# Projecting the leftover channels for both row halves side by side, and splitting the second chunk in the first slot

## What is computed

```python
# L0: 32 -> 192 -> 192 -> 32 channels, w1, w2, w3 ternarized (delta = 0.7 mean|w|)
h = relu6(bn(conv1x1(x, w1)))
h = relu6(bn(conv3x3(h, w2)))          # the largest part of the work
x = x + bn(conv1x1(h, w3))             # the projection
# L1: two 3x3 convolutions, 32 -> 32, weights and activations rounded to 8 bits
out = relu(bn(conv3x3(q(x), q(w1))))
x = relu(bn(conv3x3(q(out), q(w2))) + x)
# L2, L3: relu(bn(conv3x3(x, w) + b)), a channel whose largest value is under 1e-3 is set to zero
```

## Time and profile before

| | us |
|---|---|
| median of 3 runs | 267.81 |
| range of these | 267.43 to 267.94 |
| profiled execution | 268.13 |
| its span, first to last instruction | 266.3 |
| TensorE busy | 234.2 |
| VectorE busy | 233.2 |
| ScalarE busy | 184.2 |

### The profile page before, as it was taken

One profiled execution on the slowest core, in us unless ns is written; L12 is line 12 of the kernel. 1 busy time (PEld: TensorE's weight loads), 2 busy tenths in 40 slices (PEclk: granted clock), 3 DMA queues, 4 the chain that ended last, 5 costly groups with the idle time before them and its releaser, 6 DMA issues.

```text
span 266.3 us, 5565 instructions
## 1 busy us (share of the span) xinstructions
PE 234.2 (88%) x2151; PEld 133.3 (50%) x2151; DVE 233.2 (88%) x466; ACT 184.2 (69%) x274; POOL 8.7 (3%) x26
## 2 busy tenths in 40 slices
PE   0659999099999989999998999999997999789982
PEld 0315555056555445655454555555643555446651
DVE  3799989927999899999989999889878948999994
ACT  5799896348666467866458757969342747997962
POOL 4400000000000000000000000000000000000003
PEclk9999999859999999999999999999999999999997
DMA  7327100200002100001200000000000000254306
GB/s 238 99 62 241 40 1 15 75 2 0 2 0 70 25 0 2 1 2 32 60 2 0 4 0 0 2 2 1 0 2 1 2 0 0 55 118 103 88 19 241
DMA packets 7098, 10.72 MB, mean 40 GB/s; under 512 B 2176, under 2 KB 5216, under 8 KB 7072
## 3 DMA queue, kind: packets, MB, share of 16 engines
q1 hardware_dynamic: 6880, 10.33, 14.1%
q10 hardware_dynamic: 192, 0.04, 0.1%
HBM read 4.04 MB, written 1.61 MB: 21 GB/s over the span
## 4 chain that ended last, share of the span: by engine, by line
DVE 37%; PE 34%; issue 11%; ACT 8%; DMA 5%; SPq 3%; DVEq 0%; ACTq 0%
PE ps L533 10%; PE ps L522 5%; PE ps L708 4%; PE ps L544 4%; DVE hs L1251 3%; DVE h2a L1299 3%; PE ps L555 3%; DVE ps L1278 3%; DVE hs L1243 2%; DMA big<-w2b_in 2%; PE ps L643 2%; DVE h2a L1294 2%; DVE big L1587 1%; DVE cmx L1632 1%; DMA xk<-xpart 1%
## 5 line engine op out<-in xcount | busy, mean ns | idle before, releaser
L533 PE MATMUL ps<-vv,w2at 128*128 128x378 f16 (+1 forms) x192 | 38.2, 336 | 0.6 <-DVE ps L1278 0.6
L828 ACT ACTIVATE ra<-ps,bn 128x392 f32<-128x392 f32 x32 | 21.4, 675 | 19.9 <-PE ps L479 19.2
L522 PE MATMUL ps<-vv,wu 128*128 128x392 f16 x180 | 34.8, 329 | 0.0
L746 PE MATMUL ps<-big,wst 128*32 128x378 f16 (+10 forms) x576 | 24.5, 326 | 3.6 <-DVE big L1587 2.2
L533 PEld LDWEIGHTS ps<-vv,w2at 128*128 128x128 f16 x192 | 17.9, 99 | 15.8 <-issue 5.1
L708 PE MATMUL ps<-qi,wqi 128*128 128x378 bf16 (+7 forms) x144 | 23.9, 325 | 0.6 <-ACT qi L1027 0.6
L522 PEld LDWEIGHTS ps<-vv,wu 128*128 128x128 f16 x180 | 17.4, 98 | 12.1 <-DVE vv L1261 0.2
L860 ACT ACTIVATE hs<-ug,magic 128x784 f16<-128x784 f16 x16 | 15.2, 948 | 11.1 <-DVE ug L1232 11.1
L874 ACT ACTIVATE r2a<-ps,bn 128x784 f32<-128x784 f32 x15 | 15.1, 1003 | 10.7 <-DVE h2a L1299 10.7
L746 PEld LDWEIGHTS ps<-big,wst 128*32 128x32 f16 x576 | 15.2, 96 | 13.0 <-issue 2.2
L533 PE MATMUL ps<-vv,w2bt 128*128 128x378 f16 (+1 forms) x96 | 21.2, 330 | 0.0
(11 more groups left out here) (218 smaller groups left out, 443.6 us busy)
## 6 DMA issues: line engine op xcount, KB each, us to landing
xk<-xpart SPq DMA_DIRECT2D x45, 49.0 KB, 1.9
xin<-x_in SPq DMA_DIRECT2D x4, 392.0 KB, 3.8
big<-part SPq DMA_DIRECT2D x25, 49.0 KB, 2.0
big<-big SPq DMA_DIRECT2D x3, 392.0 KB, 3.6
y_out<-xin SPq DMA_DIRECT2D x3, 392.0 KB, 2.4
big<-w2a_in SPq DMA_DIRECT2D x3, 288.0 KB, 4.3
big<-w2b_in SPq DMA_DIRECT2D x6, 144.0 KB, 4.0
y_out<-xin SPq DMA_DIRECT2D x2, 196.0 KB, 2.4
```

The costliest lines, as they stand in the source:

```text
L522: i = nc.tensor.matmul(landing(slice(0, P), PBANK[k], dx), weights(raw, mid, k, dx, False), moving(s, k, dx, b), start=(n == 0 and dx == D ...
L533: i = nc.tensor.matmul(landing(slice(0, P), PBANK[k], dx), weights(raw, mid, k, dx, False), moving(s, k, dx, b), start=False, stop=(n == 2 ...
L746: i = nc.tensor.matmul(img(ps[C * g:C * g + C, bank + h, :W * n], n)[:, to[0], to[1]], wst[:, layer, C * t:C * t + C], kst[:, KBUF[layer][ ...
L828: nc.scalar.activation(ra[:, 0, HALF * h:HALF * h + HALF], ps[:, bank, :HALF], ACT.Relu, bias=bn[:, BSH, BN1A:BN1A + 1], scale=bn[:, BSC, ...
```

## The change

Four things are different.

1. Chunk 1 is split in slot 0: `x_high(1, 0)` behind the relu_main halves of image 2, `x_high(1, 1)` behind `relu_a(0)`, `split_second(1)` behind `split_first(1)`. Before, they stood between slots 0 and 1 and in slot 1.
2. A third group of semaphores, `s_second`, counts the transfers of a chunk's second image; `s_xk` counts the last two images. `expand_rest` of the first pair waits for the first two images alone, that of the second pair for the last two; the waits of `expand_main` on transfers go, but for image 2.
3. On ScalarE, `relu_main(j+2, 0)` of slots with g = 1 comes behind `relu_b(j-1)` and `copy_y(j)`, and `add_shift(c)` behind `relu_rest(j+3, 0)`.
4. `project(c, banks)` does both halves: all `h2a` steps of h = 0, those of h = 1, and then the `h2b` steps with the halves in turn, h = 1 two images on, so that neighbouring matmuls use different halves of the array's rows and different columns. It signals `proj_done` once, and both residuals wait for it.

```diff
-XK = [16 * 3 * (G - 2)] + [16 * 3 * (G - 1)] * (NCH - 1)
+XK = 16 * 3 * (G - 2)
...
                 for g in range(0 if c else 1, G):
+                    landed = s_first[c] if g == 0 else s_second[c] if g == 1 else s_xk[c]
                     for k in range(3):
                         sp.dma_start(xk[C * k:C * k + C, G * c + g, :],
-                                     xpart[C * g:C * g + C, c % 2, k, :]).then_inc(s_first[c] if g == (0 if c else 1) else s_xk[c], 16)
+                                     xpart[C * g:C * g + C, c % 2, k, :]).then_inc(landed, 16)
...
             def expand_main(j, h):
 
                 if h == 0:
-                    if j >= G and j % G == 0:
-                        pe.wait_ge(s_first[j // G], 48)
-                    if j == 2 or j >= G and j % G == 1:
-                        pe.wait_ge(s_xk[j // G], XK[j // G])
                     if j == 2:
+                        pe.wait_ge(s_xk[0], XK)
                         pe.wait_ge(rb_ready, 4)
...
             def expand_rest(j, h):
 
                 if h == 0:
-                    if j >= G and j % G == 0:
+                    if j % G == 0:
                         pe.wait_ge(s_first[j // G], 48)
-                        pe.wait_ge(s_xk[j // G], XK[j // G])
+                        pe.wait_ge(s_second[j // G], 48)
+                    else:
+                        pe.wait_ge(s_xk[j // G], XK)
                     pe.wait_ge(ra_ready, 2 * j if j > 2 else 6)
...
-            def project(c, h, steps=(0, 1, 2, 3), bank=7, end=False):
-
-                if bank == 6 and not end:
+            def project(c, banks, end=False):
+
+                if not end:
                     pe.wait_ge(ra_ready, 2 * (G * (c + 1) + 2) + 2)
-                wait(pe, y0_ready, (2 * c + h if end else 2 * c) if bank == 7 else 0)
-                lower = slice(HB * h, HB * h + HB)
-                for s in steps:
-                    if s == 0:
-                        pe.wait_ge(h2a_ready, (c + 1) * G + (h if end else 0))
-                    if s == (2 if end else 1):
-                        pe.wait_ge(h2_ready, (c + 1) * G)
-                    for g in range(G):
-                        w, rhs = ((w3t[:, 0, :], h2a[:, g, s, HALF * h:HALF * h + HALF]) if s < 2 else
-                                  (w3t[lower, 1, :], h2b[lower, g, s - 2, :]))
-                        i = nc.tensor.matmul(ps[C * g:C * g + C, bank, :HALF], w, rhs, start=(s == steps[0]),
-                                             stop=(s == steps[-1]))
+                wait(pe, y0_ready, 2 * c)
+                for h in range(2):
+                    pe.wait_ge(h2a_ready, (c + 1) * G + (h if end else 0))
+                    for s in range(2):
+                        for g in range(G):
+                            nc.tensor.matmul(ps[C * g:C * g + C, banks[h], :HALF], w3t[:, 0, :],
+                                             h2a[:, g, s, HALF * h:HALF * h + HALF], start=(s == 0), stop=False)
+                pe.wait_ge(h2_ready, (c + 1) * G)
+                for s in range(2):
+                    for k in range(G):
+                        for h in range(2):
+                            g = (k + 2 * h) % G
+                            lower = slice(HB * h, HB * h + HB)
+                            i = nc.tensor.matmul(ps[C * g:C * g + C, banks[h], :HALF], w3t[lower, 1, :],
+                                                 h2b[lower, g, s, :], start=False, stop=(s == 1))
                 i.then_inc(proj_done, 1)
...
-                    project(c - 1, 0, bank=6)
-                    project(c - 1, 1)
+                    project(c - 1, (6, 7))
...
-            project(NCH - 1, 0, end=True)
-            project(NCH - 1, 1, (2, 3, 0, 1), bank=6, end=True)
+            project(NCH - 1, (7, 6), end=True)
...
-                    if ahead and not even:
+                    if ahead and g == G - 1:
                         relu_main(j + 2, 0)
                     relu_b(j - 1)
                     copy_y(j)
-                    if ahead and even:
+                    if ahead and g < G - 1:
                         relu_main(j + 2, 0)
...
-                dve.wait_ge(proj_done, 2 * c + h + 1)
+                dve.wait_ge(proj_done, c + 1)
```

More of the change, by code:

```diff
@@ L209, in conv_seq @@
         s_first = [sem(f"s_first{c}") for c in range(NCH)]
+        s_second = [sem(f"s_second{c}") for c in range(NCH)]
         s_xk = [sem(f"s_xk{c}") for c in range(NCH)]
@@ L258, in wait, with spread_landed @@
                 eng.wait_ge(s, n)
+        def spread_landed(eng, c):
+            if c:
+                eng.wait_ge(s_first[c], 48)
+            eng.wait_ge(s_second[c], 48)
+            eng.wait_ge(s_xk[c], XK)
         def stack_free(eng, layer, c):
@@ L456, in expand_one @@
                 if n == 0:
-                    pe.wait_ge(s_first[0], 48)
+                    pe.wait_ge(s_second[0], 48)
                 nc.tensor.matmul(ps[:, bank, :HALF], (w1t[:, 0:P], w1t[:, P:P + 2 * HB])[two],
@@ L786, in x_high @@
                 if c >= 2:
-                    act.wait_ge(s_first[c - 2], 48)
-                    act.wait_ge(s_xk[c - 2], XK[c - 2])
+                    spread_landed(act, c - 2)
                 act.wait_ge(*((s_x[c], 16) if k == 0 else (xr_ready, c + 1)))
@@ L921, in slot @@
                 if begin:
+                    x_high(1, 0)
                     relu_rest(j + 2, 0)
@@ L937, in slot @@
                 relu_a(j)
-                if not begin:
+                if begin:
+                    x_high(1, 1)
+                else:
                     copy_m1(j + 1)
@@ L944, in slot @@
                     integer_block(after, 3)
+                if not even and j + 3 < B:
+                    relu_rest(j + 3, 0)
                 if g == 1:
                     add_shift(c)
-                if not even and j + 3 < B:
-                    relu_rest(j + 3, 0)
             act.wait_ge(bn1_ready, 1)
@@ L996, in _ @@
             slot(0, 0, first=True)
-            x_high(1, 0)
-            slot(0, 1, first=True, split=(1, 1))
+            slot(0, 1, first=True)
             slot(0, 2, first=True, split=(2, 0))
@@ L1159, in split_second @@
                 if c >= 2:
-                    dve.wait_ge(s_first[c - 2], 48)
-                    dve.wait_ge(s_xk[c - 2], XK[c - 2])
+                    spread_landed(dve, c - 2)
                 tt(xpart[:, c % 2, 2, :], xrest[:], high(xrest[:]), ALU.subtract).then_inc(x_split, 1)
@@ L1343, in slot @@
                     if g == 1:
-                        wait(dve, proj_done, 2 * c)
+                        wait(dve, proj_done, c)
                     upper_a(j - 1, (g - 1) % G)
@@ L1351, in slot @@
                     split_first(1)
+                    split_second(1)
                 if ahead and not even:
@@ L1434, in _ @@
             slot(0, 0, first=True)
-            split_second(1)
             slot(0, 1, first=True)
```

## The result

The changed kernel takes **258.92 us** (median of 4 runs, 258.72 to 259.40); the kernel before, timed beside it, 267.88 us (4 runs, 267.43 to 268.01). The ratio is 0.9671, with a 95% interval of 0.9653 to 0.9689. The forecast was 258.8, with a range of 257.0 to 261.8. The profiled execution took 259.40 us, with a span of 257.6, against 268.13 before. Two executions of the experiments fell in a slower state, 278.95 us of the variant with less VectorE work and 265.62 us of the one with the groups alone; the ratios leave such executions out.

The account below looks back on a forecast made before the run. It took TensorE and VectorE, both 88% busy, as nearly full, with VectorE setting the time up to the last slots and TensorE at the end. -7.67 - 2.58 + 0.39 + 0.88 = -8.98 us gave 258.8 us, range 257.0 to 261.8.

Parts of the forecast that it names:

- grid_main of image 4, VectorE: Slot 2: VectorE gets there 7.67 us earlier, 6.95 of waits, 0.63 from slot 1, 0.1 of rounding.
- VectorE's waits in g = 1: Slots (1,1), (2,1), (3,1): waits of 0.78, 0.78 and 1.02 us go with ScalarE's new order, 2.58 us off.
- add_shift: ScalarE, relu_rest ahead of it: TensorE's 0.93 us waits count nothing, as VectorE sets the time; bounds 0 and 1.9.
- projection inside: Three projections in the loop, each 0.54 us shorter, all eaten by TensorE's wait for the residual: 0, bounds 0 and 1.6.
- TensorE behind at the end: Last slots: TensorE's matmuls set the time; VectorE is 10.25 us early, TensorE only 9.86, so 0.39 back.
- signal at the end: Last projection: residual(3,0) waits for one signal behind everything, 0.88 us back; bounds 0.8 and 1.0.
- The hole: TensorE idle 6.42 us before chunk 1's first use, then some 2.9 us lost by the low clock; both would go.
- The wait in slot 1: TensorE's second expand_main waits about 0.55 us, as relu_main(3,0) ends at 42.45 behind relu_b and copy_y.
- Rival 1: Only the hole is repaid; the 0.78 and 1.02 us waits return as waits for relu_main: 261.0 us, chance 0.20.
- rival 3: Projection: row halves drain at each alternation, 1.65 us per projection: 263.2 us, chance 0.05.
- Rival 4: Slower than before: the clock falls behind four TensorE waits of 0.55 to 1.1 us: 270.4 us, chance 0.02.
- rival 2: Chunk 1's first use: TensorE's idle time shrinks but the clock still falls, costing 2.9 us: 261.7 us, chance 0.08.

Follow-up runs that it names:

- variant with less VectorE work: Changed kernel with the last projection as before, and without VectorE's second subtraction for chunks 2 and 3: 256.50 us, ratio 0.9561.
- groups alone: Kernel before with only the third group of semaphores, so expand_rest of image 4 waits for six transfers instead of twelve: 263.86 us, ratio 0.9864.
- two orders: Changed kernel's sixteen h2b matmuls with halves in turn, against a run with all h = 0, then all h = 1: 258.80 us in a single run.
- early split alone: Kernel before with only the split of chunk 1 moved into slot 0; TensorE still waits for all twelve transfers: 260.11 us, ratio 0.9724.
- filled hole: Kernel before with 34 matmuls of zeros into an unused bank ahead of TensorE's wait for chunk 1's transfers: 266.98 us, ratio 0.9960.
- late split: Changed kernel with chunk 1 split where it was before, behind slot 0 and in slot 1: 259.99 us, ratio 0.9731.
- GpSimd variant: Changed kernel with the last projection as before, and VectorE's four subtractions for chunks 2 and 3 on GpSimd: 259.86 us, ratio 0.9702.

## Why the prediction was right, point by point

The forecast was 258.8 and the result 258.92. The steps were right in kind, but that they agree to 0.1 us is luck in part. The medians give a gain of 8.96 us for 8.98 forecast, with some 0.5 us either way by the interval. The traces give 9.36 us up to the first residual of the end, 0.4 more than forecast, and the start-up that ran 0.66 us later hid it in the profiled execution. Shifts below are between the two traces, with the 0.66 us added.

| step | forecast | measured |
|---|---|---|
| grid_main of image 4, VectorE | -7.67 | 61.99 to 54.87: -7.78 |
| VectorE's waits in g = 1 | -2.58 | all three gone; undone, 2.1 us |
| L1297 of slot (3,1), both together | -10.25 | 178.60 to 168.61: -10.65 |
| add_shift | 0 | 0 (258.87 without it) |
| projection inside | 0 | about -0.25, at the third |
| TensorE behind at the end | +0.39 | -10.65 to -10.27 at the last `h2a`: +0.38 |
| signal at the end | +0.88 | +0.91 |
| first residual of the end | -8.98 | 200.43 to 191.73: -9.36 |

- **The hole.** The spread starts at 38.79 - 0.66 = 38.13, where 38.2 was forecast, TensorE waits for no transfer, and the clock does not fall behind it. The low clock's price in it was 2.72 us, forecast 2.9. The wait in slot 1 is 0.27 us instead of 0.55, and nothing hangs on it.
- **relu_b and copy_y first.** Rival 1 fell, since no wait for `ra` takes the place of the old ones. The one wait of VectorE for `ra` in the loop, 0.33 us at 158.47, is not new: the kernel before has the same 0.33 us at 167.37. Of the 1.02 us in slot (3,1), which the prediction put on this order whole, 0.24 belong to the projection, as the run with the relus in their old order shows.

- **add_shift.** The value, nothing, was right. The remark behind it, that the gain above would be lost again without it, was wrong: without it TensorE waits 0.51 us and no time is lost. That VectorE is the later of the two there is the prediction's own reason. The remark contradicted it.
- **Projection.** 1.23 us for 1.24 forecast (the sum as written, 4 x 0.166 + 0.11 + 2 x 0.17 + 0.11, gives 1.22), with waits of 0.96, 0.93 and 0.29 us behind it for 0.9, 1.1 and 0.2. Of the term's size the third was missed: there the saving of 0.5 us was said to be eaten whole while the wait behind it was put at 0.2, so 0.3 had to be left. The experiments found 0.25. The sum lost nothing by it, since the 1.02 us above had that part in them. The bounds (0 and 1.6) held it.
- **A drain at each alternation** (rival 3) fell by the earlier trace rows before and by the 0.46 and 0.47 us of the two orders now. The Trainium skill, TensorEngine Tiling (Array Packing), Key Properties, says that changing the tiling mode, and not just the tile, drains the engine; the runs agree, as the sixteen cost the same with one change of row half (0.47 us) or with fifteen (0.46).
- **Rival 4**, a clock that falls behind short waits: waits of 0.96, 0.93 and 0.74 us left it at its upper level in every slice of the loop. It did not happen behind the 1.07 us of the early split alone or the 1.62 us of the filled hole either, nor behind the 2.06 and 2.69 us that were traced. For the untraced runs with 2 to 2.7 us it is open, as above, so rival 2 may have been a real danger for a smaller change than this.
- **The end.** +0.91 for +0.88. It was the one term that the change could have done without, and the version without it is the fastest: 257.88 us.

Where do the 0.4 us come from? The prediction took each wait of VectorE at the length that is shown for it. A wait costs some 0.08 us more, as above, and five of them went: two ahead of grid_main(4), where the prediction had 0.1 for rounding, and three in slots with g = 1, where VectorE's shift grows by 0.87, 0.86 and 1.10 us for waits of 0.78, 0.78 and 1.02. That is 0.3 of the 0.4 us, and the rest is within what two traces differ by.

## What to carry to other kernels

A hole of an engine costs what the engines behind it wait, and where the engine is TensorE also what the lower clock takes from the work behind (2.7 us here); price both, and expect that two cures for one hole overlap. When two engines are 88% busy, find out which one never waits: its work and its waits count, and a faster form on the other one turns mostly into idle time (0.25 us of 1.6 came through here). Price a wait that goes from the starts of the instructions around it, since it takes the lost overlap with it, 0.08 us each here. Joining two results under one signal is free where their reader comes late and costs the whole difference where the reader stands waiting, so decide it place by place.

## What the runs showed of the hardware

- **GpSimd beside VectorE.** An f32 subtraction of 784 elements on GpSimd (1.5 to 2.3 us, the same 0.97 us on VectorE) held up an instruction of VectorE beside it, which then ended 0.2 to 0.8 us behind GpSimd's: 2.15 for 0.98, 1.85 for 0.77, 1.65 for 0.36, 1.39 for 0.97. Not each one was held up: a seed of 1.04 us that reads PSUM, at 37.85, and an `hs` of 0.97 us at 65.49 kept their length. The Trainium skill, GPSIMD Engine Reference, Specifications, says that the two share their SBUF interfaces, with contention for VectorE's instructions that have two SBUF inputs or run in a 2-port mode. The trace agrees for three of the four, which have two SBUF inputs; the fourth, the 1.65 us, has one, and no run shows its mode. The effect was larger than I had thought: help from GpSimd cost VectorE as much as it saved.
- **The rate of DMA issue varies.** The twelve transfers of one spread took SP 7.47 us in the kernel before, 7.48 with the late split and 7.49 in the GpSimd variant, but 8.1 to 8.7 in all other traces. TensorE being idle is not the reason, as the groups-only kernel with its 2.69 us hole took 8.16 and the GpSimd variant, with TensorE busy, 7.49. The cause is open. The issue time of a spread read from one trace can be 15% off in the next.
- **The start-up** takes another time in each execution, over a range of 1.6 us (22.02 to 23.61 us in fourteen traces), and moved all that follows by 0.66 us between the two traces above. That it is the clock's rise is inferred from the spacing of the matmuls there. Where terms of half a microsecond are compared, two traces have to be lined up behind it first.
